# Output-weight loads issued by GpSimd at the beginning of its steps instead of by SyncE

## The chip, the cores and the metric

The kernel runs on one core of a Trainium2 chip. The metric is the device time of one execution in microseconds (us), the median over several runs; lower is better. The core has five engines that run their own instruction streams and meet only at semaphores: TensorE (PE, matrix products), VectorE (DVE), ScalarE (ACT), GpSimd (POOL) and SyncE (SP), which here only issues DMAs. [...]

## The reference, cut to what matters

One layer on x of shape (4, 512, 1024), in float32:

```python
xn = layernorm(x)
q, k, v = xn @ Wq.T, xn @ Wk.T, xn @ Wv.T        # 32 query heads, 8 key/value heads, 128 wide
q, k = rmsnorm(q) * qw, rmsnorm(k) * kw
scores = q k^T / sqrt(128) + slope * (key - query), causal mask
out = softmax(scores) @ v
s = out.reshape(b, 512, 4096) @ Wo.T             # the output weights: 4096 x 1024
g = silu(xn @ W.T + bias + sum of 8 rank-16 LoRA terms)
return x + s * g
```

Wo is what the changed loads bring in.

## The kernel before, in words

**Tiles and precision.** Every float32 product is made of three products of a "hi" part (the value rounded by a copy on ScalarE) and a "lo" part (the rest: value minus hi). So each weight tile is loaded by DMA into a "lo" buffer, ScalarE copies it to a "hi" buffer, and GpSimd subtracts hi from it in place. Only then may TensorE use it.

**Stages.** After a preparation of some 130 us the program has 32 groups, n = 0 to 31 (4 batch elements times 8 key/value heads), each with four steps, j = 0 to 3, one for each query head; step number m = 4n + j. Every engine has its own function `step(n, j)`, and runs its steps in order, the instructions of a step in the order of the code. In step m TensorE does, in this order: the scores of head m with the attention product of head m - 1; some transposes; the input projections for group n + 1 (units P1 and P2 in j = 0, P6 and P7 in j = 1, P4 alone in j = 2, P5 and P3 in j = 3); the first two column blocks of the output projection of head v = m - 2; nine transposes of the probabilities (`turn_probs` of key tiles 0 to 2); the third block; the last transpose (key tile 3); the fourth block. The step j = 2 is shorter, since it has one unit. The last group has no projections.

**Input weights.** `wl` and `wh` hold four half units in a ring. SyncE loads a half unit (`load_w`, L289, 448 KB) as soon as TensorE is through with the half that it replaces; ScalarE splits it (`split_w`, L764) between the transposes at the end of its step; GpSimd's `low_w` (L1014) comes last in GpSimd's step: four of them in j = 0, 1 and 3, two in j = 2.

**Output weights.** `wb_lo` and `wb_hi` have two buffers. `load_b(v)` (L296 to L302, 512 KB) waits for `out_done`, the end of the output projection of v - 2, which is the end of TensorE's step v; in the first 32 loads also for `wo_copied`, a copy of the weights made two steps earlier (`copy_b`). It is issued in step m = v + 1 as SyncE's first instruction. In the same step ScalarE splits it (`split_b`, L774): in j = 1, 2 and 3 right after `normalise`, ahead of `square_rows` and `rsqrt`, in j = 0 after two copies of the projections. GpSimd's `low_b` (L1025) follows in the same step, and TensorE uses the buffer in the next one.

**The order on ScalarE and VectorE in step j = 2.** ScalarE: `exps`, `head_out`, `normalise`, `split_b`, six squares (L786), `rsqrt` (L803, L805), `probs_hi` for key tiles 0 to 2 (L810), two `split_w`, `probs_hi` of tile 3. VectorE: the sums of the projections, `add_out(v, 0)`, `row_factors`, which waits for `rsqrt`'s result (L1186), `add_out(v, 1)` (L1267), `probs_lo` (L1208). TensorE's last transpose (L587) takes the bank that the first of these `probs_lo` sets free.

**The order on GpSimd.** A step of GpSimd begins with `bias_of(m + 1)` (L1033, one product for the next step's scores), then `low_b`, then now and then other work, then `low_product` (L1014). In groups 0 to 5, steps j = 1 and 3, the other work is `weight_sums` (L1063 to L1068, four subtractions that prepare the weights of a later group); in j = 1 and 3 of groups 8, 16 and 24 it is `finish`.

Of the kernel before, what the change touches and what calls it, by code (L numbers as in the profile page):

```python
# [7 lines left out]
F32 = mybir.dt.float32  # L8
# [16 lines left out]
NV = NH  # L25
# [89 lines left out]
def build_layer(nc, x_tok, x_first, xT, wa, wo, wT, lora_a, lora_bt, lw, ffn_b, qw, kw, rel, slopes,  # L115
                ident, outT):
    with ExitStack() as ctx:
        def sb(name, shape, dt=F32):
            return ctx.enter_context(nc.sbuf_tensor(name, shape, dt))
# [4 lines left out]
        def sem(name):  # L124
            return ctx.enter_context(nc.semaphore(name))

        weff = nc.dram_tensor("weff", [NK, P, TILE], F32).ap()
        wo_in = nc.dram_tensor("wo_in", [HKV * 4, P, TILE], F32).ap()
# [8 lines left out]
        wb_hi, wb_lo = sb("wb_hi", [P, 2, TILE], F32R), sb("wb_lo", [P, 2, TILE], F32R)  # L137
# [33 lines left out]
        wo_copied = sem("wo_copied")  # L171
# [7 lines left out]
        b_in = [sem("b_in0"), sem("b_in1")]  # L179
# [6 lines left out]
        out_done, s_done, tr_done, pv_done, weff_done = (  # L186
            sem(n) for n in ("out_done", "s_done", "tr_done", "pv_done", "weff_done"))
# [73 lines left out]
        def need(eng, semaphore, value):  # L261
            if value > 0:
                eng.wait_ge(semaphore, value)
# [8 lines left out]
        def _(sp):  # L272
# [19 lines left out]
            def load_product(n, p):  # L292
                for h in range(2):
                    load_w(HW * n + 2 * p + h)

            def load_b(v):  # L296
                if not 0 <= v < NV:
                    return
                need(sp, out_done, 4 * v - 4)
                if v < 32:  # L300
                    sp.wait_ge(wo_copied, 16 * (v + 1))
                sp.dma_start(wb_lo[:, v % 2, :].bitcast(F32), wo_in[v % 32]).then_inc(b_in[v % 2], 16)  # L302

            def copy_b(v):
                if v < 32:
                    need(sp, wo_copied, 16 * v)
                    sp.dma_start(wo_in[v], wo[v]).then_inc(wo_copied, 16)

            def load_weights(g, h):
                for a in range(2):  # L310
                    for tile, src, at, width, c in ((2, 0, 0, 256, 0), (0, 0, 256, 128, 0),
                                                    (0, 128, 320, 128, 1), (4, 0, 64, 256, 1)):
                        rows = wa[g * 6 + tile + a].rearrange("p (k n) -> p k n", k=4)
                        sp.dma_start(prep_tile(g, h, a, c)[:, :, at:at + width],
                                     rows[:, 2 * h:2 * h + 2, src:src + width]
                                     ).then_inc(prep_in[h], 16)
# [20 lines left out]
            def store_sums(g, h):  # L337
                sp.wait_ge(prep_t[h], 4 * (g + 1))
                place = prep_place(g, h)
                kept = wu[(g * 2 + h) * NP + 3:(g * 2 + h) * NP + 7].rearrange("s p n -> p s n")  # L340
                sp.dma_start(kept, place[:, 0:4 * 896].rearrange("p (s n) -> p s n", s=4)
                             ).then_inc(prep_tst[h], 16)
# [30 lines left out]
            def store_result(b, half):  # L373
                for c in range(4 * half, 4 * half + 4):
                    sp.wait_ge(fin_done, b * NK + c + 1)
                    sp.dma_start(outT[b * NK + c], result_slots(b, c)[0]).then_inc(res_out[c % 4], 16)
# [44 lines left out]
            def step(n, j):  # L421
                b, g = divmod(n, HKV)
                new = n + 2 if n + 2 < HKV else None
                ending = b - 1 if g in (0, 1) and b > 0 else None
                load_b(4 * n + j - 1)
                copy_b(4 * n + j + 1)
                if j == 0:
                    if g == 1 and ending is not None:
                        store_result(ending, 1)
                    if n + 1 < HKV:  # L430
                        store_sums(n + 1, 1)
                    load_product(n + 1, P6)
                    load_product(n + 1, P7)
                    if new is not None:
                        sp.wait_ge(prep_tst[1], 16 * new)
                        load_weights(new, 0)
                        load_gate_weights(new, 0)
                    if n == 6:
                        load_x(1)
                if j == 1:  # L440
                    if new is not None:
                        store_halves(new, 0)
                    load_product(n + 1, P4)
                    if g == 0 and ending is not None:
                        store_result(ending, 0)
                    load_product(n + 1, P5)
                if j == 2:
                    if g == 0 and ending is not None:
                        load_result(ending, 1)
                    if new is not None:  # L450
                        store_sums(new, 0)
                    load_product(n + 1, P3)
                    if new is not None:
                        sp.wait_ge(prep_tst[0], 16 * (new + 1))
                        load_weights(new, 1)
                        load_gate_weights(new, 1)
                    if n + 1 == NG:
                        load_result(b, 0)
                        store_gate(n)
                        load_result(b, 1)  # L460
                if j == 3:
                    if new is not None:
                        store_halves(new, 1)
                    load_product(n + 2, P1)
                    load_product(n + 2, P2)
                    if n + 1 < NG:
                        store_gate(n)
                    if g == 3 and 0 < b < BATCH - 1:
                        load_x(b + 1)
                    if g == 7 and b + 1 < BATCH:  # L470
                        load_result(b, 0)

            for n in range(NG):
                for j in range(G):
                    step(n, j)
            load_b(NV - 1)
            store_result(BATCH - 1, 0)
            store_result(BATCH - 1, 1)
            for i in range(4):
# [521 lines left out]
        def _(pool):  # L1001
# [15 lines left out]
            def low_product(n, p):  # L1017
                for h in range(2):
                    low_w(HW * n + 2 * p + h)

            def low_b(v):
                if not 0 <= v < NV:
                    return
                pool.wait_ge(wb_hi_done, v + 1)
                pool.tensor_tensor(wb_lo[:, v % 2, :], wb_lo[:, v % 2, :].bitcast(F32), wb_hi[:, v % 2, :],  # L1025
                                   ALU.subtract).then_inc(wb_ready, 1)

            def bias_of(m):
                if m >= NH:
                    return  # L1030
                if m >= 2:
                    wait_alone(pool, scored, 4 * m - 4)
                pool.tensor_scalar(bias_sb[:, m % 2, :], rel_sb[:], slope[:, m % H:m % H + 1], None,  # L1033
                                   ALU.mult).then_inc(bias_ready, 1)
# [56 lines left out]
            def step(n, j):  # L1091
                b, g = divmod(n, HKV)
                m, v = 4 * n + j, 4 * n + j - 2
                next_x = b + 1 if b + 1 < BATCH else None
                bias_of(m + 1)
                if j == 0 and n + 1 == NG:
                    values_lo(n)
                low_b(v + 1)
                if (g, j) == (6, 3) and next_x is not None and b > 0:
                    x_sum(next_x, P7)  # L1100
                if (g, j) == (7, 0) and next_x is not None:
                    x_sum(next_x, P6)
                if j == 0 and n + 1 < NG:
                    values_lo(n)
                if (g, j) == (7, 0) and next_x is not None:
                    x_sum(next_x, P5)
                    x_sum(next_x, P3)
                if j in (1, 3) and n + 2 < HKV:
                    weight_sums(n + 2, j // 2)
                if g == 0 and b > 0 and j in (1, 3):  # L1110
                    finish(b - 1, j // 2)
                low_product(*[(n + 1, P6), (n + 1, P4), (n + 1, P3), (n + 2, P1)][j])
                if (g, j) == (6, 3) and b == 0:
                    x_sum(1, P7)
                if j != 2:
                    low_product(*[(n + 1, P7), (n + 1, P5), None, (n + 2, P2)][j])
                if j == 3 and n + 1 == NG:
                    for c in range(4, NK):
                        add_base(c)
# [15 lines left out]
            for n in range(NG):  # L1135
                for j in range(G):
                    step(n, j)
            low_b(NV - 1)
            for half in range(2):
                finish(BATCH - 1, half)  # L1140
# [414 lines left out]
```

## Time and profile before

| | us |
|---|---|
| median of 3 runs | 2666.16 |
| lowest and highest | 2663.68, 2668.66 |
| the profiled execution, its time | 2668.54 |
| its span in the trace | 2666.8 |
| TensorE busy in the span | 2585.4 |
| ScalarE, GpSimd, VectorE busy | 1765.1, 1714.3, 1687.0 |

The span is what the hardware profiler recorded from first to last instruction of one execution; its own time is 1.7 us longer. "Busy" counts instructions at work, and not waits or the issuing of DMAs. In the rows below a line number is that of the kernel before, `out<-in` are the tiles, `x4` merges four instructions in a row, and `[8.07 <-ACT wh L764]` says that the engine was idle for 8.07 us before it, until the instruction named had ended.

### The profile page before, as it was taken

What the parts mean: (1) busy time and instruction counts of PE and PEld (TensorE: products, weight loads), DVE (VectorE), ACT (ScalarE), POOL (GpSimd) and SP (SyncE); (2) the same over time, 40 slices, a digit from 0 to 9 for tenths busy, and PEclk for the clock granted to TensorE, in tenths of its full rate; (3) what the DMA queues carried; (4) which work ended last, traced back from release to release, by engine and by line L of the source; (5) the groups of instructions that cost most, each with busy time, mean ns of one, the idle gap of its engine ahead of it and who ended that gap; (6) DMA issues with size and microseconds to landing.
All of it is one profiled execution on the core that took longest, in us unless ns stands there. A gap on an engine that the chain in (4) does not pass through costs nothing.

```text
span 2666.8 us, 39893 instructions
## 1 busy us (share of the span) xinstructions
PE 2585.4 (97%) x13840; PEld 2292.9 (86%) x13840; DVE 1687.0 (63%) x3530; ACT 1765.1 (66%) x4635; POOL 1714.3 (64%) x839
## 2 busy tenths in 40 slices
PE   5689999999999999999999999999999999999997
PEld 4578888888888888888888888888888888888886
DVE  6446566667667656566666666656666756566666
ACT  4366667667767666667766667666767666667664
POOL 3377877886667656656667756566666756656555
PEclk9889999999999999999999999999999999999999
DMA  7788778785345333433334433433334533333323
GB/s 264 264 275 284 251 259 286 252 264 182 127 151 174 111 114 104 151 115 104 115 118 165 140 111 105 156 106 107 113 109 137 181 112 106 112 119 110 112 78 131
DMA packets 179192, 418.45 MB, mean 157 GB/s; under 512 B 31152, under 2 KB 72240, under 8 KB 178096
## 3 DMA queue, kind: packets, MB, share of 16 engines
q1 hardware_dynamic: 177728, 414.78, 48.0%
q8 instruction: 112, 1.84, 0.3%
q10 hardware_dynamic: 1264, 1.12, 0.1%
q14 instruction: 88, 0.72, 0.1%
HBM read 343.48 MB, written 89.13 MB: 162 GB/s over the span
## 4 chain that ended last, share of the span: by engine, by line
PE 91%; DVE 2%; POOL 2%; DMA 2%; ACT 2%; SPq 1%; issue 1%; POOLq 0%; DVEq 0%; ACTq 0%
PE proj L490 22%; PE proj L492 22%; PE proj L491 21%; PE tr L587 5%; PE tr L567 3%; PE sc L490 3%; PE sc L491 3%; PE sc L492 3%; PE ot L491 3%; PE ot L492 3%; PE ot L490 3%; PE tr L560 1%; DMA wl<-wu 1%; DMA wu<-xtok 0%; POOL wl L1014 0%
## 5 line engine op out<-in xcount | busy, mean ns | idle before, releaser
L1014 POOL TENSOR_TENSOR wl<-wl,wh 128x896 fp32r<-128x896 f32 x436 | 924.9, 2151 | 589.7 <-ACT wh L764 589.7
L490 PE MATMUL proj<-wh,xh 128*128 128x448 f32 x1792 | 673.3, 376 | 24.3 <-POOL wl L1014 16.6
L491 PE MATMUL proj<-wl,xh 128*128 128x448 f32 x1792 | 660.8, 369 | 0.0
L492 PE MATMUL proj<-wh,xl 128*128 128x448 f32 x1792 | 660.6, 369 | 0.0
L1025 POOL TENSOR_TENSOR wb_lo<-wb_lo,wb_hi 128x1024 fp32r<-128x1024 f32 x128 | 307.9, 2405 | 293.9 <-ACT wb_hi L774 293.9
L831 ACT ACTIVATE misc<-misc,negmax 128x128 f32<-128x128 f32 (+3 forms) x512 | 286.6, 565 | 266.6 <-DVE negmax L1243 266.6
L490 PE MATMUL proj<-o_hi,wb_hi 128*128 128x512 f32 x1024 | 424.9, 415 | 4.6 <-DVE o_lo L1254 2.5
L1267 DVE TENSOR_TENSOR acc<-acc,proj 128x512 f32<-128x512 f32 x476 | 325.7, 685 | 151.9 <-PE proj L492 150.0
L764 ACT ACTIVATE wh<-wl 128x896 fp32r<-128x896 f32 x436 | 395.2, 966 | 34.0 <-DMA wl<-wu 33.3
L810 ACT ACTIVATE pT_hi<-tr 128x512 fp32r<-128x512 f32 (+3 forms) x512 | 197.7, 440 | 327.5 <-PE tr L587 327.5
L492 PE MATMUL proj<-o_hi,wb_lo 128*128 128x512 f32 x1024 | 403.4, 394 | 0.0
L491 PE MATMUL proj<-o_lo,wb_hi 128*128 128x512 f32 x1024 | 401.0, 392 | 0.0
L1238 DVE TENSOR_TENSOR raw<-raw,proj 128x448 f32<-128x448 f32 x320 | 197.7, 618 | 308.5 <-PE proj L492 306.6
L490 PEld LDWEIGHTS proj<-wh,xh 128*128 128x128 f32 x1792 | 339.4, 189 | 55.0 <-issue 18.2
L492 PEld LDWEIGHTS proj<-wh,xl 128*128 128x128 f32 x1792 | 339.2, 189 | 30.1
L491 PEld LDWEIGHTS proj<-wl,xh 128*128 128x128 f32 x1792 | 339.7, 190 | 27.8
L1243 DVE CUSTOM_DVE_ANT_0 misc<-sc,misc 128x128 f32<-128x128 f32 (+3 forms) x512 | 240.8, 488 | 173.2 <-PE sc L492 172.4
L1208 DVE TENSOR_TENSOR pT_lo<-tr,pT_hi 128x512 fp32r<-128x512 f32 (+3 forms) x512 | 227.1, 485 | 78.1 <-ACT pT_hi L810 77.5
L786 ACT ACTIVATE junk<-raw 128x128 f32<-128x128 f32 x640 | 189.8, 300 | 110.1 <-DVE raw L1238 109.4
L838 ACT ACTIVATE misc<-misc,rs_inv 128x128 f32<-128x128 f32 (+3 forms) x512 | 245.4, 559 | 0.0
L490 PEld LDWEIGHTS proj<-o_hi,wb_hi 128*128 128x128 f32 x1024 | 193.3, 189 | 48.4 <-DVE o_lo L1254 3.7
L1033 POOL TENSOR_SCALAR misc<-misc,slope 128x512 f32<-128x512 f32 x128 | 232.8, 1818 | 0.0
(129 smaller groups left out, 4395.8 us busy)
## 6 DMA issues: line engine op xcount, KB each, us to landing
wl<-wu SPq DMA_DIRECT2D x436, 448.0 KB, 3.9
wb_lo<-wo_in SPq DMA_DIRECT2D x128, 512.0 KB, 3.3
wu<-xtok SPq DMA_DIRECT2D x13, 1792.0 KB, 10.0
wo_in<-wo SPq DMA_DIRECT2D x32, 512.0 KB, 5.7
xtok<-wa SPq DMA_DIRECT2D x52, 256.0 KB, 4.6
wu<-xtok SPq DMA_DIRECT2D x13, 896.0 KB, 5.4
gate_dram<-misc SPq DMA_DIRECT2D x32, 256.0 KB, 5.0
xtok<-xT SPq DMA_DIRECT2D x28, 256.0 KB, 5.1
```

Of the source, the lines that this page charges most:

```text
L490: pe.matmul(out, hi_l, hi_r, start=first, stop=False, skip_group_check=onto)
L491: pe.matmul(out, hi_l, lo_r, start=False, stop=False, skip_group_check=onto)
L492: return pe.matmul(out, lo_l, hi_r, start=False, stop=last, skip_group_check=onto)
L764: act.activation(w_slot(wh, w), w_slot(wl, w, True), ACT.Copy).then_inc(w_hi_done, 1)
L831: act.activation(p, p, ACT.Exp, bias=negmax[:, i:i + 1], scale=-1.0, accum_out=rowsum[:, i:i + 1]).then_inc(exp_done, 1)
L838: ins = act.activation(p, p, ACT.Copy, scale=rs_inv[:, i:i + 1])
L1014: pool.tensor_tensor(w_slot(wl, w), w_slot(wl, w, True), w_slot(wh, w), ALU.subtract).then_inc(w_ready, 1)
L1025: pool.tensor_tensor(wb_lo[:, v % 2, :], wb_lo[:, v % 2, :].bitcast(F32), wb_hi[:, v % 2, :], ALU.subtract).then_inc(wb_ready, 1)
L1033: pool.tensor_scalar(bias_sb[:, m % 2, :], rel_sb[:], slope[:, m % H:m % H + 1], None, ALU.mult).then_inc(bias_ready, 1)
L1208: dve.tensor_tensor(dst, bank, hi, ALU.subtract).then_inc(tr_free, 1)
L1243: dve.tensor_tensor_reduce(prob[:, P_AT[i]:P_AT[i] + w], sc_ps[i % 2][:, 0:w], bias_sb[:, m % 2, S - w:S], -1.0, 3e38, ALU.add, ALU.min, n ...
L1267: dve.tensor_tensor(a, a, bank, ALU.add).then_inc(out_free, 1)
```

## The change

`load_b` is no longer called in SyncE's `step`, but as the first call of GpSimd's `step`, with the same index (v + 1 with v = m - 2, which is 4n + j - 1), the same waits and the same buffers; the load of the last weights, `load_b(NV - 1)`, moves from the end of SyncE's program to GpSimd's, ahead of the last `low_b`. All other loads and stores stay with SyncE, and nothing that is computed changes.

```diff
@@ block.sync @@
-            def load_b(v):
-                if not 0 <= v < NV:
-                    return
-                need(sp, out_done, 4 * v - 4)
-                if v < 32:
-                    sp.wait_ge(wo_copied, 16 * (v + 1))
-                sp.dma_start(wb_lo[:, v % 2, :].bitcast(F32), wo_in[v % 32]).then_inc(b_in[v % 2], 16)
...
                 ending = b - 1 if g in (0, 1) and b > 0 else None
-                load_b(4 * n + j - 1)
                 copy_b(4 * n + j + 1)
...
-            load_b(NV - 1)
             store_result(BATCH - 1, 0)
@@ block.gpsimd @@
+            def load_b(v):
+                if not 0 <= v < NV:
+                    return
+                need(pool, out_done, 4 * v - 4)
+                if v < 32:
+                    pool.wait_ge(wo_copied, 16 * (v + 1))
+                pool.dma_start(wb_lo[:, v % 2, :].bitcast(F32), wo_in[v % 32]).then_inc(b_in[v % 2], 16)
...
                 next_x = b + 1 if b + 1 < BATCH else None
+                load_b(v + 1)
                 bias_of(m + 1)
...
+            load_b(NV - 1)
             low_b(NV - 1)
```

GpSimd before, in a middle group, from the end of its step j = 0 to the start of j = 3 (`misc<-misc,slope` is `bias_of`, `wb_lo` is `low_b`, `wl` is `low_w`):

```order
L1038 TENSOR_TENSOR v_lo<-raw,v_hi 128x512 [waits v_hi_done]
L1014 TENSOR_TENSOR wl<-wl,wh 128x896 [waits w_hi_done] x4
L1033 TENSOR_SCALAR misc<-misc,slope 128x512 [waits scored]
L1025 TENSOR_TENSOR wb_lo<-wb_lo,wb_hi 128x1024 [waits wb_hi_done]
L1014 TENSOR_TENSOR wl<-wl,wh 128x896 [waits w_hi_done] x4
L1033 TENSOR_SCALAR misc<-misc,slope 128x512 [waits scored]
L1025 TENSOR_TENSOR wb_lo<-wb_lo,wb_hi 128x1024 [waits wb_hi_done]
L1014 TENSOR_TENSOR wl<-wl,wh 128x896 [waits w_hi_done] x2
```

The same engine in the changed kernel, steps j = 1 (its `low_w` at the top) to j = 3 (its line numbers are those of the changed file, where L1017 is the load, L1031 `bias_of`, L1023 `low_b` and L1004 `low_w`):

```order
L1004 TENSOR_TENSOR wl<-wl,wh 128x896 [waits w_hi_done] x4
L1017 DMA wb_lo<-wo_in 128x1024 [waits out_done]
L1031 TENSOR_SCALAR misc<-misc,slope 128x512 [waits scored]
L1023 TENSOR_TENSOR wb_lo<-wb_lo,wb_hi 128x1024 [waits wb_hi_done]
L1004 TENSOR_TENSOR wl<-wl,wh 128x896 [waits w_hi_done] x2
L1017 DMA wb_lo<-wo_in 128x1024 [waits out_done]
L1031 TENSOR_SCALAR misc<-misc,slope 128x512 [waits scored]
```

The load now stands behind the two or four `low_w` of the step before it, and ahead of `bias_of`.

SyncE before, from step j = 1 to j = 0 of the next group:

```order
L302 DMA wb_lo<-wo_in 128x1024 [waits out_done]
L289 DMA wl<-wu 128x896 [waits w_half]
L289 DMA wl<-wu 128x896 [waits u_done]
L302 DMA wb_lo<-wo_in 128x1024 [waits out_done]
L289 DMA wl<-wu 128x896 [waits w_half]
L289 DMA wl<-wu 128x896 [waits u_done]
L289 DMA wl<-wu 128x896 [waits w_half]
L289 DMA wl<-wu 128x896 [waits u_done]
L359 DMA gate_dram<-misc 128x512 [waits gate_ready]
L302 DMA wb_lo<-wo_in 128x1024 [waits out_done]
```

SyncE in the changed kernel, the end of a group (the store of the gate is L351 there):

```order
L289 DMA wl<-wu 128x896 [waits w_half]
L289 DMA wl<-wu 128x896 [waits u_done]
L289 DMA wl<-wu 128x896 [waits w_half]
L289 DMA wl<-wu 128x896 [waits u_done]
L351 DMA gate_dram<-misc 128x512 [waits gate_ready]
```

Only the loads of `wb_lo` and their waits are gone from SyncE's stream; what stood behind them waits for events on TensorE as before.

## Rows read from the trace of the kernel before

**Rows 1.** The page: busy time by engine; the chain that ended last

```profile
PE 2585.4 (97%) x13840; PEld 2292.9 (86%) x13840; DVE 1687.0 (63%) x3530; ACT 1765.1 (66%) x4635; POOL 1714.3 (64%) x839
...
PE 91%; DVE 2%; POOL 2%; DMA 2%; ACT 2%; SPq 1%; issue 1%; POOLq 0%; DVEq 0%; ACTq 0%
```

**Rows 2.** SyncE's queue: line, what it waited for, total us, times, longest

```profile
SPq L302 <- PE proj L492: 711.0, 114, 20.4
```

**Rows 3.** Timeline of SyncE (start us, us, what), four steps of group 14

```profile
1235.42 0.32 SPq L302 DMA_DIRECT2D wb_lo<-wo_in  x1
...
1256.60 0.32 SPq L302 DMA_DIRECT2D wb_lo<-wo_in  x1
...
1277.78 0.32 SPq L302 DMA_DIRECT2D wb_lo<-wo_in  x1
1285.23 1.53 SPq L289 DMA_DIRECT2D wl<-wu  x2
1293.06 0.32 SPq L302 DMA_DIRECT2D wb_lo<-wo_in  x1
```

**Rows 4.** Timeline of GpSimd, same stretch

```profile
1242.52 1.57 POOL L1033 TENSOR_SCALAR misc<-misc,slope 128x512 f32<-128x512 f32 x1
...
1263.71 1.56 POOL L1033 TENSOR_SCALAR misc<-misc,slope 128x512 f32<-128x512 f32 x1
...
1285.32 1.57 POOL L1033 TENSOR_SCALAR misc<-misc,slope 128x512 f32<-128x512 f32 x1
...
1295.98 2.52 POOL L1033 TENSOR_SCALAR misc<-misc,slope 128x512 f32<-128x512 f32 x1
```

**Rows 5.** Timeline of ScalarE, same stretch

```profile
1245.99 1.05 ACT L774 ACTIVATE wb_hi<-wb_lo 128x1024 fp32r<-128x1024 f32 x1
...
1264.93 1.05 ACT L774 ACTIVATE wb_hi<-wb_lo 128x1024 fp32r<-128x1024 f32 x1
...
1274.37 0.98 ACT L810 ACTIVATE pT_hi<-tr 128x512 fp32r<-128x512 f32 x2 [3.86 <-PE tr L587]
...
1285.15 1.05 ACT L774 ACTIVATE wb_hi<-wb_lo 128x1024 fp32r<-128x1024 f32 x1
...
1302.33 1.05 ACT L774 ACTIVATE wb_hi<-wb_lo 128x1024 fp32r<-128x1024 f32 x1
```

**Rows 6.** Timelines of VectorE and TensorE, the end of that third step

```profile
1288.70 0.58 DVE L1186 TENSOR_TENSOR tmp<-rinv 128x12 f32<-128x12 f32 x1 [0.19 <-ACT rinv L805]
...
1290.33 1.48 DVE L1208 TENSOR_TENSOR pT_lo<-tr,pT_hi 128x512 fp32r<-128x512 f32 x3
...
1291.36 0.27 PE L587 MATMUL tr<-ident_sb,misc 128*128 128x128 f32 x1
```

**Rows 7.** The same place in group 30, the last: GpSimd, then ScalarE

```profile
2561.74 1.58 POOL L1033 TENSOR_SCALAR misc<-misc,slope 128x512 f32<-128x512 f32 x1
...
2561.61 1.04 ACT L774 ACTIVATE wb_hi<-wb_lo 128x1024 fp32r<-128x1024 f32 x1
```

**Rows 8.** The page: DMA issues, KB each, us from issue to landing

```profile
wl<-wu SPq DMA_DIRECT2D x436, 448.0 KB, 3.9
wb_lo<-wo_in SPq DMA_DIRECT2D x128, 512.0 KB, 3.3
```

**Rows 9.** DMA issues, in the longer list

```profile
misc<-lora_bt ACTq DMA_DIRECT2D x1, 512.0 KB, 8.2
```

**Rows 10.** SyncE in group 4, an early group; then GpSimd

```profile
462.17 0.34 SPq L333 DMA_DIRECT2D wu<-xtok  x1
...
464.76 1.58 POOL L1033 TENSOR_SCALAR misc<-misc,slope 128x512 f32<-128x512 f32 x1
467.14 2.39 POOL L1025 TENSOR_TENSOR wb_lo<-wb_lo,wb_hi 128x1024 fp32r<-128x1024 f32 x1 [0.80 <-ACT wb_hi L774]
...
486.73 1.58 POOL L1033 TENSOR_SCALAR misc<-misc,slope 128x512 f32<-128x512 f32 x1
```

**Rows 11.** Timeline of GpSimd at the program's end

```profile
2650.08 2.84 POOL L1025 TENSOR_TENSOR wb_lo<-wb_lo,wb_hi 128x1024 fp32r<-128x1024 f32 x1
```

## The prediction, made before the changed kernel was run

> **What bounds the kernel now.** I read the page first: TensorE is busy for 2585.4 of 2666.8 us, and the chain that ended last lies on it for 91% [rows 1]. So what lengthens a step of TensorE costs its full length, and what other engines do is free until TensorE waits for it. Then I read the moved instruction in SyncE's queue: 114 of its 128 issues had waited for TensorE, 711.0 us in all [rows 2]. SyncE is thus nearly always there before the condition is met, and the load goes out within some 0.2 us of the end of TensorE's step. I use its start as the mark for "a step begins". The question is when GpSimd gets to the same place, and when ScalarE wants the data. For that I laid the timelines of one middle group beside each other [rows 3 to 6]. In the changed code the load stands right where `bias_of` (L1033) begins.
>
> | step of group 14 | load on SyncE [rows 3] | GpSimd gets there [rows 4] | ScalarE begins `split_b` [rows 5] |
> |---|---|---|---|
> | j = 0 | 1235.42 | 1242.52 (+7.1) | 1245.99 (+10.6) |
> | j = 1 | 1256.60 | 1263.71 (+7.1) | 1264.93 (+8.3) |
> | j = 2 | 1277.78 | 1285.32 (+7.5) | 1285.15 (+7.4) |
> | j = 3 | 1293.06 | 1295.98 (+2.9) | 1302.33 (+9.3) |
>
> GpSimd is late because the four subtractions of the step before hold it; in j = 3 only two do. The wait for `out_done` will therefore almost never hold GpSimd, but the load itself goes out 7 us later in three steps of four. Group 30 shows the same picture in j = 2 (2561.74 on GpSimd, 2561.61 on ScalarE) [rows 7], so I take groups 6 to 30, 25 of them, as alike.
>
> **What it removes.** 128 issues of 0.32 us and their waits on SyncE [rows 3]. The next instruction there waits for a projection of the same TensorE step: it stood ready at 1277.78 and went out only at 1285.23 [rows 3]. I count nothing.
>
> **What it adds: L, from the moment GpSimd is free to the landing.** From SyncE this load takes 3.3 us [rows 8]. No row shows a DMA that GpSimd issues. The low end is the 3.3 itself; the high end is the longest row of the same size, 512 KB on ScalarE's queue in the crowded opening, 8.2 us [rows 9]. I take 4.3, near the first since transfer and destination are the same, with 1.0 us more for the issue as my estimate. In j = 2 the load now goes out at 1285.3, in the middle of a pair of 448 KB loads that SyncE issues from 1285.23 [rows 3]; before, it had the engines to itself. Such loads land after 3.9 us though they are smaller [rows 8], so I add 1.0 there as an estimate: L = 5.3 in j = 2.
>
> The Trainium skill ("DMA: Bandwidth & Descriptors", sections "Issuing engines are not separate DMA queues" and "Latency and other measured facts") speaks against any gain: an issue from another engine saves the issuing sequencer's time alone, and the first byte of a load issued by GpSimd comes after about 1 us where SyncE's comes after about 0.6. The first half agrees with SyncE's row, 0.32 us behind which nothing was late; the second no run here shows yet. An estimate by that page would be 0.4 us more than SyncE's in place of my 1.0, and a time of about 2833.
>
> **Where it is hidden.** j = 0: lands at 1242.52 + 4.3 = 1246.8, 0.8 late for ScalarE; I let the 0.8 be hidden, since what follows it there are copies that wait for TensorE. j = 1: 1268.0, 3.1 late, but ScalarE then is idle for 3.86 us before 1274.37 even in this group [rows 5], which hides it. j = 3: 1300.3, 2.0 ahead of 1302.33. If L were above 6.3, j = 3 would be late too.
>
> **Where it is not: j = 2.** The load lands at 1285.32 + 5.3 = 1290.6, while ScalarE stood ready at 1285.15: it now stands still for 5.5 us. Behind `split_b` are queued the squares and `rsqrt`; VectorE begins L1186 only with `rsqrt`'s result (idle until it, 0.19) at 1288.70; then the sum and `probs_lo` at 1290.33; its first of three ends near 1290.9 (1.48 / 3, and a little), and TensorE's last transpose, which needs its bank, began at 1291.36 [rows 6]. So 0.4 of slack and all else a chain: TensorE waits 5.5 - 0.4 = 5.1 us. After it everything is shifted by the same amount, so nothing is won back in j = 3. Sum over groups 6 to 30: 25 x 5.1 = 127.5 us.
>
> **Early groups.** In groups 0 to 5 GpSimd has `weight_sums` behind `low_b` in j = 1. In group 4 it comes to the load at 464.76, while stores that SyncE began at 462.17 are moving (L333 and the line behind it, three tiles of 448 KB) [rows 10]; I take L = 5.5 (4.3 and 1.2 for them, an estimate). `split_b` then ends 1.15 later (1.05 of work and a handover), at 471.4, and `low_b` begins there rather than at 467.14: 4.25 late. From 467.14 to 486.73 GpSimd had no idle time [rows 10], so it reaches j = 2 4.25 us later, which is added to the 5.1: 9.4 for a group, 6 x 9.4 = 56 us.
>
> **The last group.** GpSimd has no `low_w` there and comes early; the load goes out as before, and the chain has room. But the last load stands behind `add_base`. `low_b` began at 2650.08, right behind it, its data long there [rows 11]; now the load only starts there: 4.3 + 1.15 = 5.5 us later, and GpSimd's work from there to the end is one chain. 5.5 us.
>
> **Sum.** 127.5 + 56 + 5.5 = 189, on the profiled execution's 2668.5: 2857.5. The median of the runs is 2.4 lower, so I forecast **2855**. With L = 3.3 throughout: j = 2 costs 3.47 - 0.4 = 3.1, an early group 2.1 more, the end 4.5: 77.5 + 31 + 4.5 = 113, time 2779. With L = 8.2: 8.0 in j = 2 (200), 15 in an early group (90), 9 at the end, and j = 0 comes 4.7 late, of which I estimate 2 hidden (31 x 2.7 = 84): 383, time 3049.
>
> **Rivals.** (a) *The load is not late at all, and the time stays.* If GpSimd's stream can issue a DMA beside a subtraction that is still running, or ahead of the `low_w` that it is queued behind, the load goes out near +0.2 as on SyncE. It decides at +3.1 in j = 2: issued before that, it lands (4.3) before ScalarE's +7.4, and the cost is zero but for 0 to 5 us at the end: 2664 to 2671. For it: no row shows where a DMA on GpSimd stands against running work. Against it: every row of GpSimd begins only when the one before it has ended, and the load is in the same stream behind them. (b) *The landing is short*: the extra issue time and the collision are near nothing, L about 3.3 to 3.7: 2779 to 2800. For it: the transfer is the same and the DMA engines have room; against it, the pair at 1285.23. (c) *The landing is long*, above 6.5: ScalarE is late in j = 0 and j = 3 as well, 2930 to 3049. For it: GpSimd's work is the slowest per element and its `bias_of` takes 2.52 where it usually takes 1.57 [rows 4], so something already holds it up at times.
>
> The 2.52 has a rule behind it that leads to the same case: the Trainium skill ("SBUF — State Buffer", the box on "DVE blocks DMA") says that descriptors written by GpSimd wait while VectorE holds the port that both share. [...]
>
> **Chances.** The forecast's mechanism with L between those of (b) and (c): 0.70; (b) 0.13; (c) 0.09; (a) 0.08. The forecast's own range is 2800 to 2930. To leave out no more than 2 in 10 I go down to 2775, which takes in (b), and up to 2930. A difference below 0.2%, about 5 us, can't be told from no change here. Cases (b), (c) and the forecast are all slower: 0.91 with a little of (a)'s end; (a) splits into 0.06 same and 0.03 faster.
>
> **What would show it.** Right: TensorE's wait for VectorE's `pT_lo` at the last transpose of j = 2, now 0, of some 5 us, 31 times; ScalarE's `wb_hi` waiting for the DMA in j = 2 (5 us) and j = 1 (3 us) and not in j = 3; the mark of j = 3 following that of j = 2 by 20.4 us instead of 15.3; in early groups 24 or more. GpSimd's load at +7.5. Wrong: a load on GpSimd that starts before the `low_w` ahead of it ends; a landing under 3.3 or over 6.3 us; waits of TensorE in j = 0 or 1; or a TensorE whose wait in j = 2 is well below ScalarE's.

## The result, and the profile after

| | before | after |
|---|---|---|
| median (lowest to highest), us | 2667.2 (2663.68 to 2668.66) | 2901.16 (2897.42 to 2903.01) |
| span of the profiled execution | 2666.8 | 2895.6 |
| TensorE busy | 2585.4 | 2659.5 |
| TensorE idle (span less busy) | 81.4 | 236.1 |
| mean granted TensorE clock | 0.991 | 0.956 |

Four runs of each; the ratio is 1.0875 with an interval of 1.0862 to 1.0889. The change makes the kernel 234 us slower. The forecast was 2855 with a range of 2775 to 2930: the time lies in it, 46 us above the forecast.

The page of the changed kernel, the rows that answer to [rows 1] (busy time; shares of the chain that ended last), the kinds of DMA queues (packets, MB, share of 16 engines), and the landings that answer to [rows 8]:

```profile
PE 2659.5 (92%) x13840; PEld 2347.3 (81%) x13840; DVE 1652.1 (57%) x3530; ACT 1776.4 (61%) x4635; POOL 1767.6 (61%) x967
...
q1 hardware_dynamic: 159296, 347.66, 36.1%
q0 software_dynamic: 18432, 67.12, 6.7%
...
PE 63%; POOL 13%; DMA 9%; ACT 6%; issue 4%; DVE 4%; SPq 1%; POOLq 0%; ACTq 0%; DVEq 0%
...
wl<-wu SPq DMA_DIRECT2D x436, 448.0 KB, 4.2
wb_lo<-wo_in POOLq DMA_DIRECT2D x128, 512.0 KB, 3.7
```

The chain lay on TensorE for 91% before and now for 63%; GpSimd, the DMAs and ScalarE have 28% between them. TensorE executes the same 13840 matmuls and is idle for 154.7 us more (236.1 less 81.4), but it is also *busy* for 74.1 us more. The prediction has no term for the second number. GpSimd's 128 issues are counted in its busy time (967 instructions instead of 839) and travel on a queue of another kind, a software one. They land after 3.7 us in the median where SyncE's landed after 3.3.

The list of waits (who waited for whom: us in total, times, longest):

```profile
ACT wb_hi L764 <- DMA wb_lo<-wo_in: 267.6, 74, 10.2
...
DVE tmp L1186 <- ACT rinv L795: 176.2, 32, 9.4
...
PE tr L577 <- DVE pT_lo L1208: 154.5, 35, 8.7
```

This is the forecast chain: ScalarE waits for the load, VectorE for `rsqrt`, TensorE's last transpose for `pT_lo`. That last wait was 11.0 us in 7 places before, and is 154.5 in 35 now.

The places of [rows 4] to [rows 6] in the same group 14 of the changed kernel. TensorE begins its step j = 2 at 1391.3. First GpSimd, then ScalarE, VectorE and TensorE (start us, us, what; in brackets the idle time before it):

```profile
1390.23 8.80 POOL L1004 TENSOR_TENSOR wl<-wl,wh 128x896 fp32r<-128x896 f32 x4 [5.24 <-ACT wh L754]
1398.97 0.60 POOL L1017 DMA_DIRECT2D wb_lo<-wo_in  x1
1399.62 1.57 POOL L1031 TENSOR_SCALAR misc<-misc,slope 128x512 f32<-128x512 f32 x1
1404.60 2.36 POOL L1023 TENSOR_TENSOR wb_lo<-wb_lo,wb_hi 128x1024 fp32r<-128x1024 f32 x1 [3.41 <-ACT wb_hi L764]
...
1413.02 0.60 POOL L1017 DMA_DIRECT2D wb_lo<-wo_in  x1
```

```profile
1403.46 1.06 ACT L764 ACTIVATE wb_hi<-wb_lo 128x1024 fp32r<-128x1024 f32 x1 [4.47 <-DMA wb_lo<-wo_in]
...
1406.64 0.21 ACT L795 ACTIVATE rinv<-lnv 128x12 f32<-128x12 f32 x1
```

```profile
1406.89 0.17 DVE L1186 TENSOR_TENSOR tmp<-rinv 128x12 f32<-128x12 f32 x1 [4.64 <-ACT rinv L795]
...
1408.11 1.48 DVE L1208 TENSOR_TENSOR pT_lo<-tr,pT_hi 128x512 fp32r<-128x512 f32 x3
```

```profile
1408.85 0.33 PE L577 MATMUL tr<-ident_sb,misc 128*128 128x128 f32 x1 [3.59 <-DVE pT_lo L1208]
...
1412.27 0.63 PE L481 MATMUL ot<-pT_lo,v_hi 128*128 128x512 f32 x1
```

GpSimd's four `low_w` (L1004) end at 1399.0 and only then does the load start, at +7.7 in the step. ScalarE stands still for 4.47 us and begins `split_b` at +12.2 instead of +7.6 [rows 5] (both from TensorE's first product of the step, 1277.6 in the kernel before; the prediction counts from SyncE's load, 0.2 us later, and has +7.4); `rsqrt`, `row_factors` and `probs_lo` follow in the order of [rows 6]; TensorE waits 3.59. In j = 3 the load starts at 1413.02, right after the two `low_w` of j = 2, early enough for nothing to wait.

The last row is what the prediction missed. A matmul of 512 columns takes 0.39 to 0.40 us in this kernel, and this one, 3.4 us behind the wait, takes 0.63. Group 29 in three stretches: from the start of j = 2 to the end of the wait, the next 5.3 us, and the rest of j = 3 (stretch, length, busy us of TensorE, its weight loads, VectorE, ScalarE, GpSimd with counts, granted clock, DMA share, GB/s):

```profile
2687.40:2705.50 18.10, 14.00 (x76) 12.20 (x74) 7.30 (x22) 11.56 (x35) 12.23 (x7) 0.95 0.24 81
2705.50:2710.80 5.30, 5.27 (x16) 4.48 (x17) 3.30 (x10) 1.82 (x6) 5.16 (x4) 0.51 0.00 0
2710.80:2730.60 19.80, 19.80 (x109) 17.86 (x107) 11.38 (x22) 12.72 (x39) 5.32 (x3) 1.00 0.41 133
```

TensorE waited 4.13 us here before the last transpose. In the stretch behind the wait the granted clock is 0.51, which is the lower of its two levels (1.2 GHz), then it is back at 1.00 (2.4 GHz). TensorE executes 16 matmuls in those 5.3 us. So the wait is paid for, and then some of it again. It is the rule here and not the exception: in 24 of the 25 groups 6 to 30 the clock falls to the lower level in j = 2 or j = 3, in the kernel before in none of them.

Adding up the steps over the whole program (end of one step to the end of the next on TensorE, after less before) gives:

| steps | longer by | of it TensorE idle |
|---|---|---|
| groups 6 to 30, j = 2 | +137.1 | +103.5 |
| groups 6 to 30, j = 3 | +19.9 | -1.4 |
| groups 6 to 30, j = 0 and 1 | +6.3 | +4.4, in group 7 |
| groups 1 to 5, j = 2 | +52.9 | +41.6 |
| groups 1 to 5, j = 3 | +2.5 | 0 |
| group 0, j = 2 | +9.2 | +7.7 |
| the end (from TensorE's last full step) | +3.6 | +1.4 |
| all else (j = 0 and 1 of group 0 above all) | -2.7 | -2.5 |
| sum | +228.8 | +154.7 |

At the end TensorE waits 4.15 us instead of 1.23 for the last `low_b` and ends 5.1 us later, but what follows its last product is 1.4 us shorter. A typical j = 2 takes 20.8 us instead of 15.28 (the medians of 25), and the j = 3 behind it 22.2 instead of 21.18, though TensorE does not wait longer in j = 3.

### The profile page after: what moved, and what is told of

Same layout as the page of the kernel before. It is cut to its first block, busy times and chain, and to the rows that moved or that the text cites. A ratio compares the mean times of both kernels' runs of the same rounds, so it can differ in the third digit from the quotient of the medians.

```text
span 2895.6 us, 39893 instructions
## 1 busy us (share of the span) xinstructions
PE 2659.5 (92%) x13840; PEld 2347.3 (81%) x13840; DVE 1652.1 (57%) x3530; ACT 1776.4 (61%) x4635; POOL 1767.6 (61%) x967
## 4 chain that ended last, share of the span: by engine, by line
PE 63%; POOL 13%; DMA 9%; ACT 6%; issue 4%; DVE 4%; SPq 1%; POOLq 0%; ACTq 0%; DVEq 0%
PE proj L480 15%; PE proj L482 15%; PE proj L481 15%; POOL wl L1004 10%; DMA wb_lo<-wo_in 7%; PE tr L577 3%; PE tr L557 3%; PE sc L480 2%; PE sc L481 2%; PE sc L482 2%; PE ot L481 2%; PE ot L482 2%; ACT junk L776 2%; PE ot L480 2%; ACT pT_hi L800 1%
## 5 line engine op out<-in xcount | busy, mean ns | idle before, releaser
L1004 POOL TENSOR_TENSOR wl<-wl,wh 128x896 fp32r<-128x896 f32 x436 | 922.1, 2148 | 519.2 <-ACT wh L754 519.2
L480 PE MATMUL proj<-wh,xh 128*128 128x448 f32 x1792 | 674.3, 376 | 28.3 <-POOL wl L1004 20.8
L1023 POOL TENSOR_TENSOR wb_lo<-wb_lo,wb_hi 128x1024 fp32r<-128x1024 f32 x128 | 305.7, 2388 | 536.0 <-ACT wb_hi L764 536.0
L480 PE MATMUL proj<-o_hi,wb_hi 128*128 128x512 f32 x1024 | 440.6, 430 | 10.0 <-POOL wb_lo L1023 4.2
L482 PE MATMUL proj<-o_hi,wb_lo 128*128 128x512 f32 x1024 | 417.5, 408 | 0.0
L481 PE MATMUL proj<-o_lo,wb_hi 128*128 128x512 f32 x1024 | 414.2, 405 | 0.0
L577 PE MATMUL tr<-ident_sb,misc 128*128 128x128 f32 x1280 | 188.9, 277 | 159.1 <-DVE pT_lo L1208 154.5
L577 PEld LDWEIGHTS tr<-ident_sb,misc 128*128 128x128 f32 x1280 | 152.3, 141 | 195.6 <-DVE pT_lo L1208 169.2
L764 ACT ACTIVATE wb_hi<-wb_lo 128x1024 fp32r<-128x1024 f32 x128 | 135.5, 1059 | 268.5 <-DMA wb_lo<-wo_in 267.6
```

The source lines that it names most:

```text
L480: pe.matmul(out, hi_l, hi_r, start=first, stop=False, skip_group_check=onto)
L481: pe.matmul(out, hi_l, lo_r, start=False, stop=False, skip_group_check=onto)
L482: return pe.matmul(out, lo_l, hi_r, start=False, stop=last, skip_group_check=onto)
L577: mm = pe.transpose(bank[:, i * P:i * P + P], prob[:, a:a + P], ident_sb[:])
L1004: pool.tensor_tensor(w_slot(wl, w), w_slot(wl, w, True), w_slot(wh, w), ALU.subtract).then_inc(w_ready, 1)
```

## Experiments

Theory A, the prediction's: the load goes out 7.5 us late because it stands behind GpSimd's work of the step before; that lateness makes ScalarE, VectorE and TensorE wait in j = 2, and (added after the result) TensorE's clock falls behind the wait. Rival B: it is the path by which the load is issued and lands. Rival C: the load takes something from GpSimd or VectorE wherever it runs. Rival D: the +74 us of busy time is no matter of the clock. Kernels 1 to 4 ran beside 7 runs of the kernel before (median 2667.59), kernels 5 to 8 beside 9 (2667.4). "Longer by" is against the trace of the kernel before, as in the table above.

### 1. SyncE issues the loads, but as late as GpSimd does

```diff
@@ SyncE's step of the kernel before @@
+                if n + 1 < NG:
+                    last = [2 * P2 + 1, 2 * P7 + 1, 2 * P5 + 1, 2 * P3 + 1][j]
+                    sp.wait_ge(w_ready, HW * (n + 1) + last + 1 - ON_DVE)
                 load_b(4 * n + j - 1)
```

> The kernel before (SyncE issues all loads), but each load of the output weights also waits until GpSimd has ended the last subtraction of its step before, so it goes out where GpSimd issues it in the changed kernel. Theory A (the lateness in step j = 2 is the cause, with the slower clock behind TensorE's wait): TensorE waits some 3 us at the last transpose of j = 2 in 25 groups and 7 in the early ones, 2830 to 2880 us. Rival B (the cause is GpSimd's own way of issuing: 0.60 us of its time each, and a landing of 3.7 us, more beside other loads): at most 2680 us.

2855.29 us (2848.56 to 2867.35), ratio 1.0708 [1.0679, 1.0737]. Its waits, its landing, and group 29, where GpSimd's `low_w` is L1017 (SyncE, then ScalarE):

```profile
ACT wb_hi L777 <- DMA wb_lo<-wo_in: 188.6, 70, 9.4
...
PE tr L590 <- DVE pT_lo L1211: 100.2, 35, 8.1
```

```profile
wb_lo<-wo_in SPq DMA_DIRECT2D x128, 512.0 KB, 3.3
```

```profile
2656.76 0.32 SPq L302 DMA_DIRECT2D wb_lo<-wo_in  x1
```

```profile
2660.16 1.06 ACT L777 ACTIVATE wb_hi<-wb_lo 128x1024 fp32r<-128x1024 f32 x1 [3.52 <-DMA wb_lo<-wo_in]
```

The place in j = 2 is the same (+7.8 here, +7.7 in the changed kernel), the issuer is SyncE, and the time is 188 us longer where the changed kernel's is 234, as Theory A expected. Not all of the 188 is the same loss, though: SyncE held back also holds its other loads, and steps in which the changed kernel lost little are longer here, j = 1 and j = 3 of groups 1 to 5 by 12.9 and 17.3 us, and j = 3 of groups 8, 16 and 24 by 14. The comparison that is left is by j = 2: over all groups these steps are 124 us longer, of the changed kernel's 199. Lateness is the main cause. From the start of the issue to `split_b` it is 3.40 us here (2656.76 to 2660.16), and in the changed kernel 5.03 in the same group and 4.95 in the mean of groups 6 to 30. TensorE's typical wait falls from 4.0 to 2.8 us; the j = 2 steps of groups 6 to 30 are 82.7 longer instead of 137.1. So a load of GpSimd's lands about 1.4 us later in each j = 2 on top of the lateness.

Not all of that is the path. Here the load goes out 0.36 us ahead of the pair of 448 KB loads, in the changed kernel beside them (1398.97 and 1398.96 in group 14). The DMA packets in the traces tell the two parts. SyncE's load, here and in the kernel before, has its first packet 0.95 us after the start of the issue, and GpSimd's after 1.30 in j = 0, 1 and 3: 0.35 for the path. In j = 2 of the changed kernel the first packet comes after 2.28 us (medians of groups 6 to 30), while the pair's first comes after 0.93. VectorE's operations with two inputs have no part in this second delay: over all eight kernels in which GpSimd issues, 539 of its loads met no packet of another DMA 0.6 to 1.3 us after the issue, and every one had its first packet within 1.45 us, 293 of them beside a VectorE operation with two inputs in SBUF; the 200 whose first packet came after 1.6 us had all met one. So B holds for 0.35 us of the 1.4, and most of the rest goes with the packets of other loads that are already moving. No run has SyncE's own load beside the pair, so whether it would be held up as long is open.

### 2. GpSimd issues the load one place earlier

```diff
@@ GpSimd, low_product: behind the first low_w of the step before @@
                 for h in range(2):
                     low_w(HW * n + 2 * p + h)
+                    if h == 0 and load is not None:
+                        load_b(load)
...
@@ GpSimd's step; has_low tells whether the step before has a low_product @@
-                load_b(v + 1)
+                if not has_low(m - 1):
+                    load_b(v + 1)
```

> GpSimd still issues all 128 loads, but behind the first subtraction (low_w) of the step before, about 1 us after TensorE's step ends, and not behind the last one. Theory A: the data land at about +5 to +5.5 us, ahead of ScalarE's +7.4, so no wait at the last transpose of j = 2; 2662 to 2680 us, the same as before. Rival B (the way of issuing is what costs): 2850 us or more, as all 128 issues are still GpSimd's.

2712.10 us (2711.59 to 2715.13), ratio 1.0169 [1.0153, 1.0184]. 189 of the 234 us are gone with the same engine issuing, so GpSimd's issue as such is not what costs (its loads of j = 2 land after 3.7 us in the median here, at +1.4 in the step, ahead of the pair); but my 2662 to 2680 missed by over 30. `split_b` is back at +7.57 in j = 2 and TensorE hardly waits there. What is left is mostly in j = 3 (+19.7 in groups 6 to 30, against +13.9 in j = 2), where nobody had expected it. Group 14, the beginning of j = 3; `raw<-raw,tmp` is VectorE's scaling of the keys and queries, two of 128x512. GpSimd, VectorE, TensorE:

```profile
1316.67 0.61 POOL L1023 DMA_DIRECT2D wb_lo<-wo_in  x1
1317.31 2.14 POOL L1004 TENSOR_TENSOR wl<-wl,wh 128x896 fp32r<-128x896 f32 x1
```

```profile
1317.42 3.75 DVE L1206 SCALAR_TENSOR_TENSOR raw<-raw,tmp 128x512 f32<-128x512 f32 x2
```

```profile
1320.20 0.66 PE L557 MATMUL tr<-ident_sb,raw 128*128 128x128 f32 x4 [0.27 <-DVE raw L1206]
```

The same two in the kernel before, and the whole line in both (times, us, mean ns):

```profile
1294.25 2.90 DVE L1198 SCALAR_TENSOR_TENSOR raw<-raw,tmp 128x512 f32<-128x512 f32 x2
```

```profile
L1198 DVE SCALAR_TENSOR_TENSOR raw<-raw,tmp 128x512 f32<-128x512 f32 x160 | 152.6, 986 | 1.1
```

```profile
L1206 DVE SCALAR_TENSOR_TENSOR raw<-raw,tmp 128x512 f32<-128x512 f32 x160 | 180.9, 1163 | 1.1
```

The issue of 0.61 us pushes the second `low_w` on, so that it lies beside the scaling: the two operations take 3.75 us instead of 2.90, and TensorE's transposes wait for them. The mean of all 160 goes from 986 to 1163 ns. The Trainium skill ("SBUF — State Buffer", section "SBUF: two separate sides") says that a VectorE operation with two inputs in SBUF and a GpSimd operation that reads SBUF exclude each other, the later one waiting for the whole of the earlier. The rows agree: `low_w` ends at 1319.45, and the first scaling, begun at 1317.42, is over by 1320.20, some 0.7 us after that, which is what one takes alone (median 0.69). A small rest, 0.4 us in each j = 2 (13.9 in all), is not explained by this and stays open.

### 3. The changed kernel with spare matmuls where TensorE waits

In j = 2 the first half of the third block of the output projection is computed again, 5 times (11 times in groups 0 to 5), into the same bank, which the last pass overwrites.

```diff
@@ TensorE's step, before out_proj(v, 2) @@
+                    if j == 2 and n + 1 < NG:
+                        bank = proj_bank(("o", v, 2))
+                        for _ in range(5 if n > 5 else 11):
+                            out_head(v, 2, 0, bank, True)
```

> The changed kernel with useless work added on TensorE in step j = 2: the first half of block 2 of the output projection is computed 5 more times (3.45 us; 11 times in groups 0 to 5) before it is computed for good, in the place where TensorE otherwise stands still. Nothing else changes. Theory C (the 74 us more of TensorE's busy time are its clock, which falls when it stands still): no transpose or product at the slower rate in j = 2 and j = 3, 2825 to 2850 us, faster than the changed kernel by 50 to 75 us although TensorE does 120 us more work. Rival D (the longer products have another cause, such as the data arriving late or the DMA traffic): the same 2901 us or longer.

2853.30 us (2845.17 to 2854.92), ratio 1.0689 [1.0673, 1.0705], 3 us above my range. TensorE executes 573 matmuls more and the kernel is 48 us *faster* than the changed one. The page, and group 29 from the start of j = 2, then j = 3:

```profile
PE 2726.3 (96%) x14413; PEld 2399.6 (84%) x14413; DVE 1668.8 (59%) x3530; ACT 1769.5 (62%) x4635; POOL 1769.1 (62%) x967
...
PEclk9799999999999999999999999999999999999999
```

```profile
2640.50:2661.00 20.50, 19.92 (x106) 17.25 (x105) 9.65 (x27) 12.69 (x36) 14.78 (x9) 1.00 0.20 72
2661.00:2682.40 21.40, 21.40 (x116) 19.10 (x115) 13.84 (x30) 14.13 (x42) 8.91 (x6) 1.00 0.39 123
```

The clock is at 1.00 throughout both stretches. The typical j = 3 is back at 21.2 us; over groups 6 to 30, j = 3 is 0.4 shorter than before (changed kernel: 19.9 longer) and j = 2 114.7 longer (137.1). The chain of ScalarE and VectorE is where it was (`split_b` at +12.5), so the filler fills a wait that stays, and what it gives back is the clock's. D falls: what the extra busy time was, is the slower clock that comes with the wait. The clock falls in j = 2 or 3 of 1 of the 25 groups here, and in 24 of them in the changed kernel. How much that is can be worked out. The 573 spare matmuls start 0.23 us apart, 132 us in all; without them TensorE is busy for 2594, 9 more than before, where the changed kernel has 74 more. Idle time and fillers are together 249 us (117.1 and 132), 13 more than the changed kernel's 236.1. So the fillers took some 65 us of slow work away and 13 came back as longer waits, a gain of 52, which is that between the two traces; between the medians it is 48. The Trainium skill ("TensorE: Matmul & The Clock Gate", "Part 1: The HAM clock gate") describes the fall to 1.2 GHz in an idle TensorE; the granted clocks of 0.51 behind the wait and 1.00 with the wait filled agree.

### 4 and 5. SyncE issues only in j = 2; GpSimd issues only in j = 2

```diff
@@ kernel 4: SyncE's step, then GpSimd's; in kernel 5 the two conditions are exchanged @@
+                if not (j != 2):
+                    load_b(4 * n + j - 1)
...
+                if j != 2:
+                    load_b(v + 1)
```

Both have four semaphores in place of two for the landings, one for each residue of v by 4.

> SyncE issues the loads of steps j = 2 as before, GpSimd those of j = 0, 1 and 3 (96 of 128); four semaphores in place of two, one for each step of a group. Theory A: the wait at the last transpose of j = 2 is gone in all groups; what is left is the carry in groups 0 to 5, where GpSimd's late low_b in j = 1 delays the subtractions of P4 (1 to 2 us in each), and 3 us at the end: 2670 to 2690 us. Rival B: three quarters of the 234 us stay, about 2840 us.

> GpSimd issues the loads of steps j = 2 alone (32 of 128), SyncE all others: the change done in one step of four. Theory A: nearly all of the cost stays, since j = 2 is where TensorE waits; without GpSimd's load in j = 1 the carry of groups 0 to 5 is gone, so their wait falls from some 8 us to some 4.5: 2840 to 2870 us. Rival B (each issue costs its share): a quarter of the 234 us, 2725 us.

Kernel 4: 2702.49 us (2701.02 to 2703.82), ratio 1.0131 [1.0114, 1.0148], 12 above my range. Kernel 5: 2865.03 us (2862.01 to 2865.99), ratio 1.0742 [1.0725, 1.0758], as expected. One step in four carries 198 of the 234 us by itself, and with it taken out 35 are left. Kernel 5's waits and its two kinds of landing:

```profile
ACT wb_hi L775 <- DMA wb_lo<-wo_in: 155.4, 33, 10.4
...
PE tr L588 <- DVE pT_lo L1219: 133.8, 35, 8.5
```

```profile
wb_lo<-wo_in SPq DMA_DIRECT2D x96, 512.0 KB, 3.2
...
wb_lo<-wo_in POOLq DMA_DIRECT2D x32, 512.0 KB, 4.7
```

The 32 loads of j = 2 from GpSimd land after 4.7 us, where all 128 of the changed kernel have a median of 3.7. So GpSimd's loads are slower in j = 2 than elsewhere, with the pair beside them; SyncE's late load of j = 2 in kernel 1, ahead of the pair, needed 3.40 from issue to `split_b`. In kernel 5 the early steps (groups 1 to 5, j = 2) are 25.4 longer and not 52.9: half of what they cost comes from the steps before. In kernel 4, j = 2 of groups 6 to 30 is only 4.0 longer, while j = 2 of groups 1 to 5 is still 15.2 longer, 5.3 are lost in j = 0 (group 7), 3 in group 0 and 8.5 at the end. Of these 8.5, TensorE's wait for the last `low_b` is 3 (4.28 us instead of 1.23); and behind TensorE's last product the program takes 4.7 us longer to close, with a last instruction of GpSimd of 9.8 us (2.8 in the kernel before, 2.7 in the changed one), which no run explains. This closing, group 7, and the 3 us in each early j = 2, where I had expected 1 to 2, put it above my range.

### 6. The changed kernel with ScalarE's `split_b` later in j = 2

```diff
@@ ScalarE's step @@
-                elif not last:
+                elif not last and j != 2:
                     split_b(v + 1)
...
-                if last:
+                if last or j == 2:
                     split_b(v + 1)
                 probs_hi(m, 3)
```

> The changed kernel with one call moved on ScalarE: in j = 2, split_b stands behind the first three probs_hi and no longer ahead of the squares and rsqrt. Loads, engines and times of issue are as in the changed kernel. Theory E (what costs is not the late data but what is queued behind the waiting ScalarE): the last transpose of j = 2 waits for less than 1 us, 2680 to 2720 us, the rest being groups 0 to 5. Rival F (TensorE, or GpSimd's low_b and low_w, need the data themselves): 2800 us or more.

2771.79 us (2769.50 to 2776.43), ratio 1.0393 [1.0379, 1.0408], some 50 above my range. The wait of j = 2 is gone (15.28 us typical, +1.3 over groups 6 to 30), and 130 us with it. Neither theory had the time, 2680 to 2720 or 2800 and more. New waits took its place in the next step:

```profile
PE sc L480 <- DVE negmax L1243: 36.8, 36, 5.4
...
PE tr L557 <- DVE raw L1198: 33.6, 30, 1.1
```

```profile
L1198 DVE SCALAR_TENSOR_TENSOR raw<-raw,tmp 128x512 f32<-128x512 f32 x160 | 194.5, 1247 | 1.1
```

j = 3 takes 23.07 us instead of 21.18. GpSimd's `low_b` and `low_w` are now as late as ScalarE's split, so GpSimd reaches j = 3 at +8.1, and its subtractions lie beside VectorE's scaling, which takes 1247 ns in the mean (986 before, 800 in the changed kernel). The transposes wait for it, 1.13 us in group 14, where the scores wait 0.46 for VectorE's `negmax` besides. That GpSimd's work itself would move had no place in my expectation.

### 7 and 8. Two ways to lose little

Kernel 7 is kernel 2 with the load of j = 3 at the beginning of the step again. In kernel 8 SyncE issues in j = 1 and 2 and GpSimd in j = 0 and 3. In both the last load goes ahead of `add_base`.

```diff
@@ kernel 7, GpSimd @@
+                if j == 3 or not has_low(m - 1):
+                    load_b(v + 1)
...
+                            v + 2 if has_low(m) and j != 2 else None)
@@ kernel 8, GpSimd; SyncE has the other two @@
+                if j in (0, 3):
+                    load_b(v + 1)
@@ both, GpSimd, last group @@
+                    load_b(NV - 1)
                     for c in range(4, NK):
                         add_base(c)
```

> The variant with loads behind the first subtraction (2712 us) with the load of j = 3 put back at the beginning of GpSimd's step, and the very last load ahead of add_base. In that variant VectorE's scaling of two row blocks in j = 3 takes 3.75 us where it takes 2.90 before, and j = 3 is 0.8 us longer, 25 times. Theory G (GpSimd's issue moved its second subtraction into the time of VectorE's operation with two inputs in SBUF, and one holds up the other): j = 3 back to 21.2 us, 2685 to 2695 us. Rival H (the 0.8 us are not from the place of that load): 2708 us, the 3 to 4 us of the last load won alone.

> As the variant in which SyncE issues in j = 2 (2702 us), but SyncE issues in j = 1 as well, so GpSimd has those of j = 0 and j = 3 (64 of 128); and the very last load stands ahead of add_base. Theory of the carry (GpSimd's late load in j = 1 delays low_b, the weight sums and P4 in groups 1 to 5, 3 us a group, and the last load costs 3 to 4 us): 2680 to 2686 us. Rival: the 15 us of groups 1 to 5 come from GpSimd's loads in j = 0 or 3, and stay: 2698 us.

Kernel 7: 2686.83 us (2684.36 to 2687.68), ratio 1.0071 [1.0058, 1.0084]. Kernel 8: 2681.15 us (2679.98 to 2688.41), ratio 1.0057 [1.0043, 1.0071]. Both as expected. Kernel 7's line of the scaling:

```profile
L1206 DVE SCALAR_TENSOR_TENSOR raw<-raw,tmp 128x512 f32<-128x512 f32 x160 | 141.7, 917 | 1.1
```

With the load out of the way the scaling is no longer stretched, and j = 3 costs nothing more (-1.4 over groups 6 to 30); the 25 us between kernels 2 and 7 lay there and at the end. What kernel 7 still loses is nearly all in j = 2, 13.6 us in groups 6 to 30, the same small rest as in kernel 2. In kernel 8 j = 2 of groups 1 to 5 costs 0.1 more than before; in kernel 4, where GpSimd issued in j = 1 as well, it was 15.2. That shows where the carry of the early groups comes from: the late load of j = 1. (The changed kernel's 52.9 has the late load of j = 2 too; kernel 5, with that one alone, has 25.4.) What kernel 8 still loses is 9 us in j = 0 of groups 6 and 7, and 4 at the end. No version beats the kernel before, and none pointed to one that would.

## Why the prediction was right

**The place and the queue: right.** The load waits for the last `low_w`, +7.7 from the start of TensorE's step, as [rows 4] have it (+7.5 from SyncE's load, which came 0.2 later). Rival (a), a load that goes out beside running work, is refuted by the rows of group 14, and kernel 1 shows that this lateness makes most of the loss in j = 2, 124 of 199 us.

**Where it is hidden: right but for one group.** j = 1 and j = 3 of groups 6 to 30 hold no new wait, and j = 0 only in group 7, where it took 6.9 us from the load's start to `split_b` and TensorE lost 4.4.

**L and the slack in j = 2: each term a little too large.** From issue to `split_b` it took 4.95 us in the mean and not 5.3. The extra for the issue was 0.4 rather than 1.0 in the median of all loads, but in j = 2 the load landed 1.4 later than SyncE's of kernel 1, of my two estimates' 2.0: 0.35 for the path and most of the rest for the pair of 448 KB loads, so the 1.0 set down for the pair was about right and the 1.0 for the issue too large. The estimate of 0.4 that the prediction worked out from the Trainium skill ("DMA: Bandwidth & Descriptors", section "Latency and other measured facts") agrees with the medians, 3.7 against 3.3, and with the first packets, 1.30 against 0.95. The slack was 1.0 and not 0.4: `split_b` of group 29 is 5.13 later than in the kernel before and TensorE waits 4.13. Half of that is a shorter chain. From the start of `split_b` to that of `probs_lo` it took 5.18 us before (1285.15 to 1290.33) [rows 5, 6] and 4.65 in group 14 of the changed kernel (1403.46 to 1408.11), and 0.41 of the difference is L1186, 0.17 us instead of 0.58: before, it ended when GpSimd's `low_b` did (1289.3), and now `low_b` is all but through (1407.0) when it begins. (The prediction's 1.48 / 3 for the first of the three `probs_lo` also takes for equal what isn't: they have 512, 384 and 256 columns.) So 103.5 us of idle time in place of 127.5.

**Two smaller points.** No load of GpSimd's was seen to wait for VectorE's port, which the prediction brings up under (c): the packets above speak for the other loads alone. And its last split of the chances has 0.91 and 0.09 for what its list has as 0.92 and 0.08.

**Early groups: 49 us of idle time instead of 56, by another split.** In group 4 `low_b` of j = 1 came 2.2 us later in the step, not 4.25 (from the load's start to `split_b` 3.5 us passed, so the stores beside it did not matter); in j = 2 the load then started at +10.1 and took 6.9 to `split_b`, not 5.3. The end cost 3.6 and not 5.5.

**The missing term: TensorE's clock, about 74 us.** The sum was made of waits alone, with the sentence that behind the wait "everything is shifted by the same amount". It isn't: behind a wait of some 4 us TensorE works at half its clock, in group 29 for 5.3 us. The idle terms predicted 189 and gave 155; the clock added 74. The two errors have opposite signs, and the forecast is closer than its working: with all idle terms right it would have said 2668.5 + 155 - 2.4 = 2821. That it came within 46 us is in part luck, and the range held the time because it was made wide for L, not because it knew of the clock. The trace of the kernel before could have warned: over its first 260 us, in which TensorE is idle for 62, the granted clock is 0.91, and from there on, where it hardly waits, 1.00.

## What to carry to other kernels

An instruction moved to another engine takes the place in that engine's queue, behind all that still runs there; read when that engine gets to the place and when the consumer wants the data, at each of the kinds of step, and expect one of them to carry the loss. When a change makes TensorE wait for several us at a time, price each wait with the slower matmuls behind it, here about half of the wait again. A late buffer also moves the work of the engine that prepares it, and that can collide with a third engine in the next step.

## What was not expected of the hardware

- Behind TensorE's wait of 4.13 us the granted clock was 0.51 over the next 5.3 us (16 matmuls, 0.63 instead of 0.39 us for 512 columns); behind the 2.64 us of kernel 1 in the same group it stayed at 1.00 (2664 to 2672 us), and behind its 2.61 us in group 14 it was 0.74 over the stretch with the wait and what follows (1400 to 1406.5). In kernel 1 it fell in 12 of the 25 groups, in the changed kernel in 24. A shorter wait can cost the clock too, or not.
- A load of GpSimd's that went out beside a pair of SyncE's had its first packet 2.28 us after the issue instead of 1.30, in the median; once begun, its own packets were no slower (144 ns each, about 170 in the steps without the pair), though all of them took 2.2 us instead of 1.9.
- A load of 512 KB keeps GpSimd itself for 0.60 us (570 to 755 ns), where SyncE's issue took 0.32 of an engine that had nothing else to do.
- Two of VectorE's two-input operations of 128x512 took 3.75 us instead of 2.90 when they lay beside more of GpSimd's subtractions (kernel 2); in the mean of 160 the same line took 800 ns in the changed kernel and 1247 in kernel 6, which differ by one call on ScalarE.
